# Down projection by tokens in a gated RWKV + quantised FFN kernel: another split of the quantisation between ScalarE and VectorE

## The reference, cut to what matters

```
def _act_fake_quant(x, clip_factor):
    scale = sigmoid(clip_factor) * max(abs(x)) / 127
    return clip(round(x / scale), -128, 127) * scale
x  = x + tanh(g_xattn) * birwkv(layernorm(x), ctx, ctx, w, u)
xq = _act_fake_quant(layernorm(x), clip_x)
h  = silu(xq @ q(w_gate).T) * (xq @ q(w_up).T)      # 4096 tokens x 704
h  = _act_fake_quant(h, clip_down)                  # needs the maximum over all of h
x  = x + tanh(g_ffn) * (h @ q(w_down).T)            # q: weights rounded to int8 steps by row
```

## Time and profile before

| What | Value |
|---|---|
| Median of 3 runs | 218.35 us (218.22 to 220.37) |
| The profiled execution's own time | 217.56 us |
| Its span, first to last instruction | 215.6 us |
| Busy over the span | DVE 170.5 us (79%), PE 169.9 (79%), ACT 155.7 (72%), POOL 137.4 (64%) |
| Mean granted TensorE clock | 0.93 |
| Share of the chain of waits | PE 36%, DVE 25%, ACT 14%, DMA 9% |

### The profile page before, as it was taken

The page is one execution under the profiler, slowest core; times in us unless marked ns, Lnnn a source line. Parts: engine busy times, 40 slices in busy tenths (PEclk is TensorE's granted clock), DMA queues, the critical chain, the costliest instruction groups (busy, mean ns, idle before and its releaser), DMA issues.

```text
span 215.6 us, 3369 instructions
## 1 busy us (share of the span) xinstructions
PE 169.9 (79%) x1121; PEld 122.7 (57%) x1126; DVE 170.5 (79%) x345; ACT 155.7 (72%) x235; POOL 137.4 (64%) x157
## 2 busy tenths in 40 slices
PE   4599977959899999972078888599799924989950
PEld 4456527959899999962056553234243403756620
DVE  0769495537657689997689679997999998999992
ACT  3459698573996996996479978578798844899400
POOL 3364223469399999884688807749887750039991
PEclk9969999999999999999556999999999995899995
DMA  3999999999999996300000000000000000004458
GB/s 98 341 371 348 348 319 292 287 292 298 289 320 252 267 243 177 101 0 2 0 0 0 0 3 2 0 0 0 3 0 0 0 0 0 3 0 146 167 195 273
DMA packets 43327, 29.30 MB, mean 136 GB/s; under 512 B 2224, under 2 KB 43056, under 8 KB 43312
## 3 DMA queue, kind: packets, MB, share of 16 engines
q1 hardware_dynamic: 43168, 28.84, 46.7%
q10 hardware_dynamic: 144, 0.26, 0.3%
HBM read 24.65 MB, written 4.46 MB: 135 GB/s over the span
## 4 chain that ended last, share of the span: by engine, by line
PE 36%; DVE 25%; ACT 14%; DMA 9%; issue 7%; POOL 3%; SPq 1%; DVEq 1%; ACTq 0%
PE ps L909 10%; PE ps L1002 9%; PE ps L1035 8%; DMA hidden<-lag_w 6%; PE ps L893 5%; DVE hidden L799 4%; DMA hidden<-in_ctx 3%; ACT hidden L504 3%; DVE h_space L856 2%; DVE hidden L817 2%; PE ps L940 2%; DVE h_peaks L828 2%; ACT silu_out L623 2%; ACT hidden L575 2%; DVE bn L679 2%
## 5 line engine op out<-in xcount | busy, mean ns | idle before, releaser
L909 PE MATMUL ps<-hidden 128*128 128x128 f32 (+1 forms) x512 | 58.7, 276 | 6.3 <-DMA hidden<-lag_w 3.0
L909 PEld LDWEIGHTS ps<-hidden 128*128 128x128 f32 x512 | 57.8, 192 | 7.6 <-issue 3.3
L397 POOL TENSOR_TENSOR x_all<-x_all,silu_out 128x512 f32<-128x512 f32 x16 | 24.3, 1526 | 8.2 <-DVE silu_out L715 8.2
L828 DVE TENSOR_REDUCE h_peaks<-hidden (+2 forms) x24 | 26.0, 1123 | 2.0 <-POOL hidden L440 1.3
L1035 PE MATMUL ps<-wdT,z_t 128*128 128x256 bf16 (+1 forms) x192 | 25.0, 285 | 2.9 <-ACT z_t L637 2.9
L706 DVE SCALAR_TENSOR_TENSOR h_space<-z_t,ps 128x256 f32<-128x256 f32 x32 | 18.9, 595 | 8.9 <-PE ps L909 8.7
L637 ACT ACTIVATE z_t<-h_space 128x1024 bf16<-128x1024 int8 (+3 forms) x12 | 20.1, 1754 | 6.8 <-DVE h_space L856 6.8
L1035 PEld LDWEIGHTS ps<-wdT,z_t 128*128 128x128 bf16 (+1 forms) x192 | 17.0, 101 | 10.8 <-issue 4.8
L623 ACT ACTIVATE silu_out<-ps,mix_scale 128x1024 f32<-128x1024 f32 (+1 forms) x18 | 18.3, 1019 | 5.8 <-PE ps L1002 3.4
L933 PE MATMUL ps<-ident,hidden 128*128 128x128 f32 x64 | 11.6, 342 | 12.6 <-POOL hidden L421 11.1
L453 POOL TENSOR_TENSOR x_all<-x_all,z_t 128x512 f32<-128x512 f32 x6 | 10.7, 1802 | 15.5 <-DVE z_t L874 15.5
(11 more groups left out here) (105 smaller groups left out, 357.2 us busy)
## 6 DMA issues: line engine op xcount, KB each, us to landing
hidden<-lag_w SPq DMA_DIRECT2D x26, 512.0 KB, 7.3
x_all<-in_x SPq DMA_DIRECT2D x8, 512.0 KB, 8.8
hidden<-in_ctx SPq DMA_DIRECT2D x8, 512.0 KB, 9.0
out<-x_all SPq DMA_DIRECT2D x16, 256.0 KB, 2.4
xq<-in_L_ffn_w_down SPq DMA_DIRECT2D x1, 704.0 KB, 5.9
xq<-in_L_ffn_w_gate SPq DMA_DIRECT2D x1, 640.0 KB, 6.9
h_space<-in_L_ffn_w_up SPq DMA_DIRECT2D x1, 640.0 KB, 6.0
lag_w<-up_out ACTq DMA_DIRECT2D x1, 255.0 KB, 7.2
```

What stands on the lines that cost most here:

```text
L397: nc.gpsimd.tensor_tensor(xs, xs, mixed[:, m % 2, :, :].rearrange("p c b -> p b c"), ALU.add).then_inc(s["x1_done"], 1)
L828: nc.vector.tensor_reduce(h_peaks[:, bass.ds(KA * b + k, 1)], hidden[:, bass.ds(b * HB + k * BT, cols)], AX.X, ALU.max, apply_absolute_val ...
L909: last = nc.tensor.matmul(ps[:, j % BANKS, c * 2 * SEQS:end * 2 * SEQS], lag_tile(j)[:, c, :], ekp[:, (j * CK + c) * 2 * SEQS:(j * CK + en ...
```

## The change

ScalarE now quantises most of h itself, straight from float32 into 16-bit whole numbers in the space of `hq`, and DVE clips these to -128..127 and casts them to bfloat16 in place. `h8` goes; `hq` has three blocks. The pieces are now cut by tokens (256 tokens of all five full tiles in blocks 0 and 1, 512 in blocks 2 and 3), the half tile of a block is a piece of its own. DVE does the scaling of four pieces (`BY_DVE`): the three for the first output and block 1's half tile. PE computes the outputs one after the other, each in its own bank of eight. `wdT` has one more tile, and the two half tiles of the weights are padded with zeros by POOL so that all matmuls use 128 rows. DVE casts pieces up to two outputs ahead of each eviction. `dve_sums` are 11, 13, 14, 15, their stores are issued by ACT's queue, the others by SP's. PE computes the row of scales earlier, and has 14 idle products before and 6 behind the transpose of the maximum.

```
-        hq = z_flat[:, 0:HB].bitcast(BF16).rearrange("p (s n) -> p s n", s=2)
+        hq = [z_flat[:, 0:HB // 2].bitcast(BF16), z_flat[:, HB // 2:HB].bitcast(BF16), h8_space[:, :].bitcast(BF16)]
-        h8 = h8_space[:, :].bitcast(I8).rearrange("p (s n) -> p s n", s=2)
...
+        OUTS = BT // 256
+        HALF_TILE = (KI, KA, 0, BT // 2)
+        FIRST = [(0, 2, 0, 256), (2, KI, 0, 256), HALF_TILE]
+        PIECES = [[*FIRST, *[(0, KI, i * 256, (i + 1) * 256) for i in range(1, OUTS)]],
+                  [HALF_TILE, *[(0, KI, i * 256, (i + 1) * 256) for i in range(OUTS)]]] \
+            + [[HALF_TILE, (0, KI, 0, BT // 2), (0, KI, BT // 2, BT)]] * (BLOCKS - 2)
+        FLAT = [(b, *p) for b in range(BLOCKS) for p in PIECES[b]]
+        BY_DVE = [FLAT.index((0, *p)) for p in FIRST] + [FLAT.index((1, *HALF_TILE))]
+        BY_ACT = [n for n in range(len(FLAT)) if n not in BY_DVE]
...
-        dve_sums = [n for n in range(SUMS) if n >= SUMS - 8 and n % 4 >= 2]
+        dve_sums = [11, 13, 14, 15]
...
 # POOL
+            pool.wait_ge(s["sc1_done"], GROUPS)
+            nc.gpsimd.memset(wdT[IR:P, KI, :], 0.0).then_inc(s["pad_set"], 1)
+            pool.wait_ge(s["pad_set"], 1)
+            nc.gpsimd.memset(wdT[0:IR, KA, :], 0.0).then_inc(s["pad_set"], 1)
+            pool.wait_ge(s["pad_set"], 2)
...
 # ACT, keep_weights(2)
+                    nc.scalar.activation(wdT[:, 0:KI, :].rearrange("p k (h n) -> p h k n", n=P), banks[:, :, 0:KI, :], ACT.Copy)
+                    for h, rows in enumerate((slice(0, IR), slice(IR, P))):
+                        last = nc.scalar.activation(wdT[rows, KI + h, :].rearrange("p (h n) -> p h n", n=P),
+                                                    banks[rows, :, KI, :], ACT.Copy)
...
 # ACT, down stage
-                    nc.scalar.activation(hq[:, b % 2, cols], h8[:, b % 2, cols], ACT.Copy).then_inc(s["hq_done"], 1)
+            act.wait_ge(s["inv_done"], 1)
+            for n in BY_ACT:
+                b, piece = FLAT[n][0], FLAT[n][1:]
+                if b >= 3:
+                    act.wait_ge(s["down_done"], OUTS * (b - 2))
+                nc.scalar.activation(part(hq[b % 3].bitcast(I16), piece), part(hidden[:, b * HB:(b + 1) * HB], piece), ACT.Copy,
+                                     scale=S["inv_h"]).then_inc(s["h_int"], 1)
+            for i, n in enumerate(dve_sums):
+                act.wait_ge(s["dve_sum_done"], i + 1)
+                act.dma_start(out_v[:, 2 * n:2 * n + 2, :], seqs(x_all, 2 * n, 2)).then_inc(s["out_done"], 16)
...
 # DVE
+            def cast_h(n):
+                ...
+                nc.vector.tensor_scalar(part(hq[b % 3], piece), part(hq[b % 3].bitcast(I16), piece), QMAX, -QMAX - 1.0,
+                                        ALU.min, ALU.max).then_inc(s["hq_done"], 1)
...
+            for n in range(len(FIRST)):
+                quantise_h(n)
+                cast_h(n)
+                cast += 1
+            cast_h(cast)
+            cast += 1
+            scale_row()
+            quantise_h(BY_DVE[-1])
+            for n in range(SUMS):
+                while cast < needed(min(n + 2, SUMS - 1)):
+                    cast_h(cast)
+                    cast += 1
+                evict(n)
+                if n in dve_sums:
+                    add_rest(n)
...
 # PE
+            pe.wait_ge(s["h_odd"], ODD * (BLOCKS + 1) - 1)
+            for h in range(CH):
+                last = nc.tensor.matmul(ps[:, 5, h * P:(h + 1) * P], ones[:, :], down_diag[:, h, :], start=True, stop=True)
+            last.then_inc(s["row_ps"], 1)
+            idle_last(14)
             pe.wait_ge(s["h_odd"], ODD * (BLOCKS + 1))
             every_partition("h_top")
+            idle_last(6)
+            def down(n):
+                b, i = n // OUTS, n % OUTS
+                ...
+                if n >= 8:
+                    pe.wait_ge(s["ffn_done"], n - 7)
+                for k in range(KA):
+                    if n == 0 and k in (0, 2, KI):
+                        pe.wait_ge(s["hq_done"], (0, 2, KI).index(k) + 1)
+                    elif k == 0:
+                        pe.wait_ge(s["hq_done"], needed(n))
+                    for j in range(2):
+                        tok = i * 256 + j * P
+                        if k < KI:
+                            at_, tile = k * BT + tok, k
+                        else:
+                            at_, tile = KI * BT + tok % (BT // 2), KI + tok // (BT // 2)
+                        last = nc.tensor.matmul(ps[:, n % 8, j * C:(j + 1) * C], hq[b % 3][:, at_:at_ + P], wdT[:, tile, :],
+                                                start=(k == 0 and j == 0), stop=(k == KA - 1), skip_group_check=True)
+                last.then_inc(s["down_done"], 1)
```

More of the change, by code:

```diff
@@ L28 @@
 I8 = mybir.dt.int8
+I16 = mybir.dt.int16
 P = 128
@@ L80, in gated_rwkv_ffn @@
         wuT = sb("wuT", [P, CH, KA * P], BF16)
-        wdT = sb("wdT", [P, KA, C], BF16)
+        wdT = sb("wdT", [P, KA + 1, C], BF16)
         w_scale = sb("w_scale", [P, 2, KA])
@@ L160, in z_bank, with part, needed @@
             return (2, 6, 0)[g % 3]
[L162 to L168, removed]
+        OUTS = BT // 256
[7 more added lines that the diff above has]
+        BY_ACT = [n for n in range(len(FLAT)) if n not in BY_DVE]
+        def part(space, piece):
+            k, end, first, last = piece
+            if k == KI:
+                return space[:, KI * BT + first:KI * BT + last]
+            return space[:, 0:KI * BT].rearrange("p (k n) -> p k n", n=BT)[:, k:end, first:last]
+        def needed(n):
+            b, i = n // OUTS, n % OUTS
+            return 1 + max(m for m, (at_, k, _, first, _) in enumerate(FLAT)
+                           if at_ == b and (k == KI or first < (i + 1) * 256))
         EVEN = (KA + 1) // 2
@@ L320, in _ @@
                     load_values("cld", clip_down)
[L322 to L326, removed]
+            for i, n in enumerate(pool_sums):
+                sp.wait_ge(s["sum_done"], i + 1)
                 sp.dma_start(out_v[:, 2 * n:2 * n + 2, :], seqs(x_all, 2 * n, 2)).then_inc(s["out_done"], 16)
@@ L848, in _ @@
             global_peak(h_peaks[:, :], "h_top", S["sgd"], S["s_h"], S["inv_h"])
[L850 to L881, removed]
@@ new lines, in _, with quantise_h @@
+            nc.vector.sem_inc(s["inv_done"], 1)
+            def quantise_h(n):
+                b, piece = FLAT[n][0], FLAT[n][1:]
+                nc.vector.tensor_scalar(part(hq[b % 3].bitcast(I16), piece), part(hidden[:, b * HB:(b + 1) * HB], piece),
+                                        S["inv_h"], None, ALU.mult).then_inc(s["h_int_own"], 1)
+            def cast_h(n):
+                b, piece = FLAT[n][0], FLAT[n][1:]
+                if n in BY_DVE:
+                    dve.wait_ge(s["h_int_own"], BY_DVE.index(n) + 1)
+                else:
+                    dve.wait_ge(s["h_int"], BY_ACT.index(n) + 1)
+                nc.vector.tensor_scalar(part(hq[b % 3], piece), part(hq[b % 3].bitcast(I16), piece), QMAX, -QMAX - 1.0,
+                                        ALU.min, ALU.max).then_inc(s["hq_done"], 1)
@@ new lines, in scale_row, with evict @@
+            def scale_row():
+                dve.wait_ge(s["tanh_done"], 2)
+                link(nc.vector.tensor_tensor(S["out_scale"], S["s_h"], S["tanh_f"], ALU.mult))
+                dve.wait_ge(s["row_ps"], 1)
+                for j in range(2):
+                    link(nc.vector.tensor_scalar(down_row[:, j, :], ps[:, 5, 0:C], S["out_scale"], None, ALU.mult))
+            def evict(n):
+                dve.wait_ge(s["down_done"], n + 1)
+                wait(dve, s["sum_done"], len([i for i in pool_sums if i <= n - 8]))
+                nc.vector.tensor_tensor(ffn[n // 4 % 2][:, n % 4, :].rearrange("p (j c) -> p j c", c=C),
+                                        ps[:, n % 8, :].rearrange("p (j c) -> p j c", c=C),
+                                        down_row[:, :, :], ALU.mult).then_inc(s["ffn_done"], 1)
@@ new lines, in add_rest @@
+            def add_rest(n):
+                dve.wait_ge(s["ffn_done"], n + 1)
+                xs = x_all[:, n * 2 * C:(n + 1) * 2 * C]
+                nc.vector.tensor_tensor(xs, xs, ffn[n // 4 % 2][:, n % 4, :], ALU.add).then_inc(s["dve_sum_done"], 1)
+            cast = 0
+            for n in range(len(FIRST)):
[6 more added lines that the diff above has]
+            quantise_h(BY_DVE[-1])
@@ L1007, in _, with idle_last @@
                 gate_up(b)
+            def idle_last(n):
+                for i in range(n):
+                    nc.tensor.matmul(ps[:, 7, :], ident_b[:, :], wgT[:, 0, 0:512], start=True, stop=True)
+            pe.wait_ge(s["h_odd"], ODD * (BLOCKS + 1) - 1)
[3 more added lines that the diff above has]
+            idle_last(14)
             pe.wait_ge(s["h_odd"], ODD * (BLOCKS + 1))
@@ L1010, in _ @@
             every_partition("h_top")
[L1012 to L1039, removed]
@@ L1041, in _ @@
-            for b in range(BLOCKS):
```

(19 more changed lines are left out.)

14 lines of the change are left out of this document (4 added, 10 removed).

## The result

The changed kernel takes 217.36 us (median of 20 runs, 215.62 to 219.26) against 218.65 us for the kernel before (20 runs): ratio 0.9929, 95% interval 0.9905 to 0.9954, that is 1.0 to 2.1 us less. The forecast was 216.9 us, range 212.0 to 220.6, most likely within 1%. The profiled execution took 216.14 us with a span of 214.3 (before 217.56 and 215.6).

A forecast was written before the change was run, and what follows sets the result against it. VectorE and TensorE were taken as level bounds of the down stage; 23.4 + 6.2 + 0.9 us from 180.1 ends it at 210.6, 1.1 us earlier, tail 0.4 shorter, 1.5 us off: 216.9 us, range 212.0 to 220.6.

The forecast's parts named there:

- A: Likeliest case for the down stage: 0.26 ns per element casts, 6.2 us queueing with POOL; 216.9 us, chance 0.52.
- B: Rival in the down stage: short casts slip between POOL's additions, queueing costs 1.7 us, not 6.2; 212.4 us, chance 0.22.
- C: Rival in the down stage: VectorE's cast goes by elements, not bytes, adding 5.9 us; 222.8 us, chance 0.18.
- signs of being wrong: Down stage: ScalarE or TensorE ending VectorE's eviction waits, POOL's additions overlapping casts, or a start later than 180.13.
- The turns: Down stage: VectorE waits for POOL's 12 additions at the shared port pair, 6.2 us, bounds 1.7 and 13.4.
- the 9.3 us: VectorE's waiting for POOL in the down stage, if locked out for a whole 1.26 us addition plus 0.115 us delay.
- VectorE's own work: Down stage: quantisations 2.1, casts 8.1, row 1.2, evictions 9.6 and additions 2.4, together 23.4 us.
- The waits: Down stage: VectorE waiting for late pieces of ScalarE and for TensorE's last outputs, 0.9 us, bounds 0.3 and 2.6.
- The tail: Time after the last addition: 3.5 us instead of 3.96, with traffic the same 16 stores.
- second queue: Stores at the end: ScalarE issues four, so 0.4 us of queueing on SyncE goes.
- Case D: Rival in the down stage: TensorE stays at 1.2 GHz for three outputs, 36 matmuls 0.105 us dearer; 218.4 us, chance 0.08.
- The early edits: Ahead of the stage: w_down stored in three instructions, two POOL memsets; cost nothing, without cover up to 0.6 and 1.3 us.

The follow-up runs named there:

- e1: Changed kernel with GpSimd adding only 8 of the 512 columns of each of its 12 outputs; ratio to the kernel before 0.9616, stage 25.42 us.
- e8: Kernel before the change with GpSimd adding only 8 of the 512 columns of each of its outputs; ratio 0.9920, stage 29.83 us.
- e7: Changed kernel with all 16 stores issued from SyncE in output order; ratio to the kernel before 0.9931, stage 31.37 us, tail 2.8 us.
- e2: Changed kernel with the half tile multiplied on 64 rows again, padding unused; ratio to the kernel before 0.9928, stage 31.38 us.
- e3: Changed kernel without the 14 and 6 idle products; ratio to the kernel before 0.9913, stage 31.38 us.
- e4: Changed kernel with each GpSimd addition split into two of 256 columns; ratio to the kernel before 0.9822, stage 29.12 us.

## Why the prediction was right, and where its sum was not

**The likeliest case, A, is what happened.** Casts of half the price per element, a queue between VectorE and POOL (at the pair of ports of the prediction) that takes back what the split saved, and nothing else in the chain. B is out: the casts did not slip between POOL's additions (802 ns on average against 548). C is out: 548 ns for 1280 elements is the byte rate (0.55 predicted), not 0.88. One of the prediction's signs of being wrong did come up, the stage starting later than 180.13; it was 0.19 us, and other profiles of either order start up to 3.8 us later.

**The turns** were put at 12 x (1.12 - 0.60) = 6.2 us. Their kind is right, their size partly luck. In the changed kernel the turns stretch VectorE by 7.3 us (e1, by groups), 1.1 more than forecast. Eleven of its instructions are stretched, not twelve, and by very different amounts. Four casts that stand behind an eviction wait 0.36 us each, less than the 0.52 forecast for each. Three casts that follow directly on the cast of a half tile, with no eviction between them to hide the addition, wait 1.06 us each, and the other four instructions 0.57 to 0.84. The two casts from 187.10 on, the first behind an eviction and the second behind the first, take 2.19 us, and 0.75 without POOL's load. The formula hides one eviction in every addition and did not see the three. The stage itself loses only 5.95 us to POOL's load, since without that load other waits appear; the nearness of 6.2 to 5.95 is no measure of the formula. The old order's stage loses 1.7 us (e8).

The rule of the Trainium skill ("SBUF — State Buffer", section "SBUF: two separate sides") is borne out in kind, the casts wait for whole additions; the 9.3 us worked out from its delay would have been off by 2.0 us, so for the size the measurement decides.

**VectorE's own work** was put at 23.4 us and is 31.37 - 7.3 = 24.1. It is not the casts: start to start the seventeen come to 8.1 us in e1, as forecast, because those of 2560 elements are dearer (0.87 us instead of 0.80) and those of 512 cheaper (0.20 instead of 0.26). Most of the rest is in evictions and additions: an addition starts 0.71 us behind the eviction it depends on (208.96 to 209.67), not 0.60, four times, and the last one is not hidden by anything behind it (0.69). The quantisation of 768 elements takes 745 ns, not 620.

**The waits** for ScalarE and TensorE were put at 0.9 us and are nothing in the changed kernel; they appear in e1, where POOL is out of the way. So three errors, +0.7, +1.1 and -0.9, make the 0.9 us between a stage of 30.5 us forecast and 31.37 measured.

**The tail** was put at 3.5 us and is 2.6. I gave the second queue 0.4; it has 0.2 (e7), and the larger part, 1.2 us, comes from stores that no longer bunch. I had put down "traffic is the same 16 stores" and looked at their number, not at how they arrive. The two errors, 0.9 us each, cancel, and that is luck: 1.1 + 0.4 = 1.5 us forecast, 0.2 + 1.4 = 1.6 measured, and 1.0 to 2.1 in the timed runs. The size of the gain was right; where it comes from was not: most of it was forecast in the stage and is in the tail.

**TensorE.** I said that the padding is hidden under DVE (shown, e2: no change) and that the first products start at 181.0 and the first eviction at 185.2; they start at 181.28 and 185.44 in a stage that began 0.19 later. A padded block takes 5.54 us instead of 6.13 (e2). Within an output the products start 0.109 us apart, not 0.105.

**The clock.** The idle products do keep it at 2.4 GHz, as expected. Case D's price, 1.5 us, was wrong: without them (e3) the clock was at 1.2 GHz until 188 and the stage as long as ever. D priced each of 36 products 0.105 us dearer and counted VectorE's row and quantisations as cover. But TensorE has slack of its own, it waits for casts in between (0.43 and 0.61 us before 182.32 and 185.59): its second output ended 6.4 us into the stage instead of 4.7 (184.98), so 1.8 us late and not 3.8 us. VectorE came for it only 6.2 us into the stage, which leaves 0.3 us, and the queue with POOL behind it took these up.

**ScalarE** is done at 199.65 (forecast 199.6):

```profile
197.23 2.42 ACT L660 ACTIVATE z_t<-hidden,small 128x2560 int16<-128x2560 f32 x1
```

The early edits show nothing: stage and tail together gained 1.6 us, and the timed runs 1.0 to 2.1; a cost of some tenths ahead of the stage could hide in that interval.

## What to carry to other kernels

When a rewrite gives an engine cheaper but more frequent instructions that take turns with another engine's, as VectorE's casts and POOL's additions do here, count the meetings, not the busy time: each costs the time of the other's instruction, less what the waiting engine has to do in front of it that takes no turns (here an eviction: 0.36 us of waiting with one, 1.06 without). It may then pay to keep two such instructions from standing behind each other, which was not tried. Making the other engine's instructions smaller helps only where that engine has time to spare (halves: 2.25 us here, a loss in the old order); first look at who really ends the stage. And a stage that ends at the same moment can still give time back in the tail, if its stores come evenly.

## What the runs showed of the hardware that I had not expected

- The cast from int16 to bfloat16 in place is not one line in the number of elements: alone (e1) 512 take 282 to 296 ns, 768 as three runs of 256 take 424, 1280 as five take 548, 2560 as five of 512 take 954. From 1280 to 2560 that is 0.32 ns per element, above the 0.26 assumed; over all seventeen casts the differences cancel.
- An addition on POOL of half the columns costs more than half: where the next follows undisturbed, 0.69 us start to start (e4), and 0.77 on average beside VectorE's casts, instead of 0.62, half of 1.23.
- The stage of 31.4 us repeats to 0.01 us over builds and runs, while its start moves by up to 3.8 us. Nearly all of the spread in these profiles lies ahead of it.
